# Attention with the keys on the partitions, no transposes of the probabilities, and the value products last in each quarter of a group

## The reference

```
# attention a
q, k, v = (einsum('bsm,hmd->bhsd', ln(x), kernel[i]) for i in range(3))
attn = softmax(einsum('bhsd,bhtd->bhst', q, k) * scale)      # 1024 x 1024 for each head
x = x + einsum(out(attn, v), WO)
# attention b: low-rank projections, and a rotary turn of q and k
q = rope((c_q @ w_up_q.T) ...); k = rope((c_kv @ w_up_k.T) ...); v = c_kv @ w_up_v.T
x = x + (softmax(q k^T / 8) v) @ w_out.T + ln(x)
# rope: even and odd features of a head: e*cos - o*sin, e*sin + o*cos
# FFN: x + gelu(ln(x) @ w1 + b1) @ w2 + b2
```

## Time and profile before

| | us |
|---|---|
| median of 3 runs | 4415.12 |
| profiled execution | 4415.62 |
| its span, first to last instruction | 4413.8 |
| PE busy | 4169.7 (94%) |
| DVE / ACT / POOL busy | 3175.3 / 2636.0 / 780.0 |
| attention a (103 to 2057) / attention b (2404 to 4199) | 1954 / 1795 |
| mean granted TensorE clock | 0.977 |

### The profile page before, as it was taken

One profiled execution on the slowest core, in us unless ns is written; L12 is line 12 of the kernel. 1 busy time (PEld: TensorE's weight loads), 2 busy tenths in 40 slices (PEclk: granted clock), 3 DMA queues, 4 the chain that ended last, 5 costly groups with the idle time before them and its releaser, 6 DMA issues. The chain is left out here.

```text
span 4413.8 us, 82276 instructions
## 1 busy us (share of the span) xinstructions
PE 4169.7 (94%) x26976; PEld 3087.3 (70%) x26976; DVE 3175.3 (72%) x5320; ACT 2636.0 (60%) x4844; POOL 780.0 (18%) x691
## 2 busy tenths in 40 slices
PE   3999999999999999998885999999999999999989
PEld 3777777777777777776773777777777767777678
DVE  5777666776667777675665888888888888888744
ACT  1665555555655565555442666666666666666644
POOL 2000000000000000001222222222222222222111
PEclk9999999999999999999997999999999999999999
DMA  5333332332223332220013333333333333333110
GB/s 178 85 87 87 86 75 65 87 87 63 71 76 87 87 81 71 74 59 24 20 39 107 103 102 99 99 99 99 101 101 101 102 100 102 100 102 99 39 35 24
DMA packets 191926, 364.02 MB, mean 82 GB/s; under 512 B 32833, under 2 KB 57665, under 8 KB 187585
## 3 DMA queue, kind: packets, MB, share of 16 engines
q1 hardware_dynamic: 187456, 351.94, 30.8%
q10 hardware_dynamic: 4224, 8.39, 0.5%
HBM read 104.34 MB, written 20.97 MB: 28 GB/s over the span
## 5 line engine op out<-in xcount | busy, mean ns | idle before, releaser
L837 ACT ACTIVATE a_pT<-a_ps_t 128x512 f32<-128x512 f32 x1024 | 557.5, 595 | 737.8 <-PE a_ps_t L662 737.7
L773 DVE TENSOR_REDUCE a_nmax<-a_ps_s 128x1 f32<-128x1024 f32 x512 | 625.0, 1221 | 389.3 <-PE a_ps_s L652 385.6
L837 ACT ACTIVATE b_pT<-b_ps_t 128x512 f32<-128x512 f32 x1024 | 556.2, 595 | 529.6 <-PE b_ps_t L662 529.6
L773 DVE TENSOR_REDUCE b_nmax<-b_ps_s 128x1 f32<-128x1024 f32 x512 | 623.1, 1217 | 273.7 <-PE b_ps_s L652 272.9
L842 ACT ACTIVATE a_p<-a_ps_s,a_nmax 128x1024 f32<-128x1024 f32 x512 | 572.7, 1119 | 53.4 <-DVE a_nmax L773 50.4
L842 ACT ACTIVATE b_p<-b_ps_s,b_nmax 128x1024 f32<-128x1024 f32 x512 | 572.5, 1118 | 40.1 <-DVE b_nmax L773 35.2
L678 PE MATMUL b_ps_o<-b_pT,b_v 128*64 128x256 f32 x4096 | 555.1, 392 | 1.5 <-issue 1.0
L678 PE MATMUL a_ps_o<-a_pT,a_v 128*64 128x256 f32 x4096 | 555.3, 392 | 1.0 <-issue 1.0
L662 PE MATMUL a_ps_t<-ident,a_p 128*128 128x128 f32 x4096 | 540.2, 276 | 3.5 <-DVE a_p L777 3.5
L662 PEld LDWEIGHTS a_ps_t<-ident,a_p 128*128 128x128 f32 x4096 | 486.4, 142 | 76.8 <-DVE a_p L777 4.8
L662 PE MATMUL b_ps_t<-ident,b_p 128*128 128x128 f32 x4096 | 531.6, 273 | 4.6 <-DVE b_p L777 4.4
(11 more groups left out here) (154 smaller groups left out, 6300.2 us busy)
## 6 DMA issues: line engine op xcount, KB each, us to landing
feat<-feat_a SPq DMA_DIRECT2D x16, 2048.0 KB, 7.8
a_q_h<-a_nat_h SPq DMA_DIRECT2D x256, 128.0 KB, 2.3
a_q_l<-a_nat_l SPq DMA_DIRECT2D x256, 128.0 KB, 2.4
feat<-feat_b SPq DMA_DIRECT2D x16, 2048.0 KB, 9.3
b_partner<-b_plain SPq DMA_DIRECT2D x256, 128.0 KB, 2.0
b_q_h<-b_nat_h SPq DMA_DIRECT2D x256, 128.0 KB, 2.3
b_q_l<-b_nat_l SPq DMA_DIRECT2D x256, 128.0 KB, 2.3
a_k_s<-a_nat_h SPq DMA_DIRECT2D x128, 128.0 KB, 2.3
```

Source lines behind the costliest of these rows:

```text
L773: dve.reduce_max(nmax[:, c % NM:c % NM + 1], ps_s[:, c % 2, :], AX_X, negate=True).then_inc(s_max, 1)
L837: act.activation(pT[:, g % 2, head, 4 * h:4 * h + 4, qi * P:(qi + 1) * P], ps_t[:, h, :, :], ACT.Copy).then_inc(s_tev, 1)
```

## The change

The function `attention` is rewritten; the FFNs and the features' first layer stay.

- Scores with the keys on the partitions: 128 keys x 512 queries of one head (`scores`), two products each, over 128 rows. A row of constant ones in `k2` against a row of -max in `q2` subtracts the maximum inside the product. So the exponentials (ACT, 128x512) come out in the layout that the value products want; the transposes, their copies, and the passes of DVE over p are gone.
- The maxima come from extra products with the queries on the partitions (`maxima`), high parts only, 64 rows each; DVE reduces them (L780), and SP brings them to one row of `q2` by DMA (`shift`).
- The sums: POOL adds the eight tiles of p (`pool_window`, seven 128x1024 additions a group), PE sums over the keys with a product by ones (`row_sums`), and reciprocal, spreading over partitions and the product with o follow, by four DMAs, DVE and POOL.
- The output projection of 512 queries is four plain float32 products in place of twelve in fp32r.
- The rotary turn is done by DVE in PSUM (`rotate`), four operations, without swaps by DMA.
- A group is now 512 queries of two heads; a window u is a group; a body has four windows, a window has four quarters b. In `pe_window` a quarter is: maxima, scores, maxima, projections, output projection, values of the quarter before, row sums.
- ACT converts high parts and keeps v; DVE makes low parts.

```diff
@@ attention: PE @@
+        def maxima(pe, t, c):
+            ...
+            pe.wait_ge(s_red, due(t, 32, c))
+            cols = slice(qi, BLOCK, BT)
+            pe.matmul(ps_x[:, 0, :], q1[0:D, slot, head, cols], k1[0:D, pair % 2, head, 0:BLOCK],
+                      start=True, stop=True).then_inc(s_m, 1)
+            pe.matmul(ps_x[:, 1, :], q1[D:P, slot, head, cols], k2[D:P, pair % 2, head, BLOCK:S],
+                      start=True, stop=True).then_inc(s_m, 1)
+        def scores(pe, t, u, b):
+            if b == 0:
+                pe.wait_ge(s_shift, due(t, 128, 32 * (u + 1)))
+            for i in range(4):
+                pe.wait_ge(s_exp, due(t, 64, e - (0, 3, 3, 2)[i]))
+                pe.matmul(ps_s[:, i % 3, :], k1[:, par, head, keys], q1[:, slot, head, :], start=True, stop=False)
+                pe.matmul(ps_s[:, i % 3, :], k2[:, par, head, keys], q2[:, slot, head, :],
+                          start=False, stop=True).then_inc(s_s, 1)
+        def out_project(pe, t, g, half):
+            ...
+            pe.wait_ge(s_x, due(t, 8, 2 * g + half))
+        def project_qk(pe, t, u, n):
+            ...
+            pe.wait_ge(s_nat_l, due(t, 8, n))
+        def project_v(pe, t, u, n):
+            if n % 2 == 0:
+                pe.wait_ge(s_nat_l, due(t, 8, 2 * u + 8))
+            ...
         def pe_window(pe, t, u):
-            for s in range(STEPS):
-                    scores(pe, t, c)
-                    transposes(pe, t, c - T_LAG)
-                    out_project(pe, t, u, s, g)
-                    project_qk(pe, t, u, s, unit_steps[s])
-                    project_v(pe, t, u, s, v_at(t)[s])
-                    pv(pe, t, g, j)
+            for b in range(4):
+                c = 8 * (u + 1) + 2 * b + 1
+                if live(t, 32, c, 8 * NGROUP):
+                    maxima(pe, t, c)
+                if live(t, 4, u, NGROUP):
+                    scores(pe, t, u, b)
+                if live(t, 32, c + 1, 8 * NGROUP):
+                    maxima(pe, t, c + 1)
+                n = units(u, b)
+                if n is not None and live(t, 8, n, 4 * NPAIR):
+                    project_qk(pe, t, u, n)
+                n = v_units(u, b)
+                if n is not None and live(t, 1, 1, BODIES):
+                    project_v(pe, t, u, n)
+                if b >= 2 and live(t, 4, u - 2, NGROUP):
+                    out_project(pe, t, u - 2, b - 2)
+                w, bb = (u, b - 1) if b else (u - 1, 3)
+                if live(t, 4, w, NGROUP):
+                    values(pe, t, w, bb)
+                if b == 1 and live(t, 4, u - 1, NGROUP):
+                    row_sums(pe, t, u - 1)
@@ attention: DVE @@
+        def rotate(dve, t, n):
+            dve.wait_ge(s_unit, due(t, 8, n + 1))
+            dve.tensor_tensor(turn[0:D, :], ps_t[D:P, 0, :], sin_t[D:P, cols], ALU.mult).then_inc(s_turn, 1)
+            dve.tensor_tensor(turn[D:P, :], ps_t[0:D, 0, :], sin_t[0:D, cols], ALU.mult).then_inc(s_turn, 1)
+            dve.wait_ge(s_turn, due(t, 32, 4 * n + 2))
+            dve.tensor_tensor(ps_t[:, 0, :], ps_t[:, 0, :], cos_t[:, cols], ALU.mult).then_inc(s_turn, 1)
+            dve.wait_ge(s_turn, due(t, 32, 4 * n + 3))
+            dve.tensor_tensor(ps_t[:, 0, :], ps_t[:, 0, :], turn[:], ALU.add).then_inc(s_turn, 1)
+        def dve_window(dve, t, u):
+            for b in range(4):
+                ...
+                    reduce(dve, t, c)
+                if b == 3 and live(t, 4, u - 1, NGROUP):
+                    ...
+                    dve.reciprocal(rqi[:], rq[:]).then_inc(s_recip, 1)
+                if converting and rope is not None:
+                    rotate(dve, t, n)
+                if converting and rope is None:
+                    convert_lo(dve, t, n)
+                    ...
+                    reduce(dve, t, c + 1)
+                if converting and rope is not None:
+                    convert_lo(dve, t, n)
+                if b == 3 and live(t, 4, u - 2, NGROUP):
+                    add_out(dve, t, u - 2, 0)
+                ...
@@ attention: POOL, SP @@
+                        pool.tensor_tensor(out, p[:, 0, 0, :], p[:, 0, 1, :], ALU.add).then_inc(s_sum, 1)
+                    ...
+                            pool.tensor_tensor(out, out, p[:, bb, i, :], ALU.add).then_inc(s_sum, 1)
+            pool.memset(k2[0:D, :, :, :].bitcast(F32), 0.0).then_inc(s_init, 1)
+            pool.memset(q2[0:D, :, :, :].bitcast(F32), 0.0).then_inc(s_init, 1)
+            if u == 0 and live(t, 1, 1, BODIES) and live(t, 1, 0, BODIES):
+                sp.dma_start(feat[:].bitcast(F32), scratch[source].bitcast(F32)).then_inc(s_feat, 16)
+            if live(t, 4, u + 1, NGROUP):
+                sp.wait_ge(s_red, due(t, 32, 8 * (u + 2)))
+                shift(sp, u + 1, 0)
```

More of the change, by code:

```diff
@@ new lines, in maxima @@
+        def maxima(pe, t, c):
+            g, qi, head = c // 8, (c % 8) // 2, c % 2
+            pair, slot = g // 2, g % 4
+            if c % 8 == 0:
+                if g % 2 == 0:
+                    for half in range(2):
+                        pe.wait_ge(s_stack[half], due(t, 2 * SD, SD * (pair + 1)))
+                pe.wait_ge(s_stack[2 + g % 2], due(t, 2 * SD, SD * (pair + 1)))
+            pe.wait_ge(s_red, due(t, 32, c))
[4 more added lines that the diff above has]
+                      start=True, stop=True).then_inc(s_m, 1)
@@ new lines, in values @@
+        def values(pe, t, w, b):
+            par = (w // 2) % 2
+            pe.wait_ge(s_exp, due(t, 64, 16 * w + 4 * (b + 1)))
+            if b == 0:
+                pe.wait_ge(s_oraw, due(t, 4, w))
+                if par == 1:
+                    pe.wait_ge(s_vmove, due(t, 1, w // 4 + 1))
+            if par == 0:
+                pe.wait_ge(s_v, due(t, 8, 8 * (w // 4) + 2 * (b + 1)))
+            for i in range(2):
+                kt = 2 * b + i
+                for head in (i, 1 - i):
@@ new lines, in out_project @@
+        def out_project(pe, t, g, half):
+            par = (g // 2) % 2
+            pe.wait_ge(s_norm, due(t, 4, g + 1))
+            pe.wait_ge(s_wor, due(t, 32, 16 * (g // 2 + 1)))
+            if half == 0:
+                pe.wait_ge(s_rb, due(t, 4, g + 2 if live(t, 4, g + 1, NGROUP) else g + 1))
+            pe.wait_ge(s_x, due(t, 8, 2 * g + half))
+            for i in range(2):
+                qi = 2 * half + i
+                mm = pe.matmul(ps_t[:, 1, i * E:(i + 1) * E], o[:, g % 2, qi * P:(qi + 1) * P], wo[:, par, :],
+                               start=True, stop=True)
+            mm.then_inc(s_o, 1)
@@ new lines, in convert_lo, with add_out @@
+        def convert_lo(dve, t, n):
+            half, which = n % 2, (n % 4) // 2
+            dve.wait_ge(s_nat_h, due(t, 8, n + 1))
+            dve.scalar_tensor_tensor(nat_l[:, half, :], ps_t[:, 0, :], scale if which == 1 else 1.0,
+                                     nat_h[:, half, :].bitcast(F32), ALU.mult, ALU.subtract).then_inc(s_nat_l, 1)
+        def add_out(dve, t, g, half):
+            dve.wait_ge(s_o, due(t, 8, 2 * g + half + 1))
+            body = t + g // 4
+            xs = tile_of(x, (body // (PAIRS // 2)) * KT + 4 * (g % 2) + 2 * half, 2)
+            dve.tensor_tensor(xs, xs, ps_t[:, 1, :], ALU.add).then_inc(s_x, 1)
@@ L953, in attention, with run @@
+        def run(eng, window):
+            for u in range(4):
+                window(eng, -1, u)
+            for u in range(4):
+                window(eng, 0, u)
+            with eng.Fori(1, BODIES - 1) as t:
+                for u in range(4):
+                    window(eng, t, u)
+            for u in range(4):
+                window(eng, BODIES - 1, u)
+            for u in range(3):
+                window(eng, BODIES, u)
         block = ctx.enter_context(nc.Block())
@@ L1020, in rope_tables @@
     sin = np.concatenate([np.sin(freqs), np.sin(freqs)], -1)[:, ::2]
[L1021 to L1023 removed]
+    row = np.arange(P)
+    sign = np.where(row < D, 1.0, -1.0).astype(np.float32)
+    pick = (row % D) // 2
     return np.ascontiguousarray(np.stack([cos.T[pick], sin.T[pick] * sign[:, None]]).astype(np.float32))
```

632 lines of the change are left out of this document (272 added, 360 removed).

## The result

The changed kernel takes 5045.1 us (median of 4 runs, 5038.1 to 5051.7) against 4414.3 for the kernel before beside it (4405.5 to 4417.0): a ratio of 1.143, with a 95% interval of 1.141 to 1.146. I had said 4850, from 4560 to 5040. The sign and the mechanism were right, the size was not: +622 us of span where I had +438. The profiled execution took 5038.1 us.

A forecast was written before the change was run, and what follows sets the result against it. PE's work and the waits PE meets were taken as the bound. Bodies -165 and +200, clock +192 and +35, DMA +108, edges +68 gave +438 on 4415.6 us: 4850 us, range 4560 to 5040.

The forecast's parts named there:

- The sign and the mechanism: Whole kernel: slower, chance 0.87, because PE stands waiting for DVE with ready value products queued behind.
- PE's own work: PE in both attentions without waits: bodies of 102.4 us in a and 94.2 in b, some 16.5 less than before.
- M: Price on PE of a pair of 64-row maxima products running side by side: 0.37 us, bounds 0.37 and 0.58.
- rival C: Maxima on PE run one after the other, 0.21 us more each: +94 and +80 us, 5025 us; chance 0.15.
- 8x0.23+0.11 = 1.95: Price on PE of a quarter's eight score products, 0.11 of it for edges: 1.95 us.
- The values' place: PE queue: ready values wait behind operations needing DVE; stalls of 3.6 us in b, 0.6 to 2.0 in quarter 3.
- The clock: TensorE's clock falls behind stalls: 2.0 us lost per 3.6 us stall, +192, and +35 for gaps of 2.0.
- Rival B: Stalls come as computed, but the clock holds amid dense work: 4590 us; chance 0.17.
- Feat and the shifts: Window 0's feat reload delays the next window's shifts: stall of 5.2 us in b, 15 times, +108 with clock.
- POOL as a bound: POOL's additions take 3.4 us and more, over 31 us a group: 4950 to 5100 us; chance 0.04.
- Edges: Starts and ends of the attentions: +22 and +30 us before the first score, +8 at each end; +68 in all.
- the old loop's edge: Loop-edge time of the earlier kernel, kept in the forecast for both attentions: 50 us in a, 27 in b.

The follow-up runs named there:

- max_same_rows: Changed kernel with both products of a maxima pair in the same 64 rows of the array, one after the other; one execution, 5280.9 us.
- max_contiguous: Changed kernel with, in attention a alone, 128 neighbouring columns of q as maxima weights instead of every fourth; one execution, 5005.1 us.
- values_ahead: Changed kernel with PE's value products moved ahead of the projections and output projection; 4588.4 us, 1.040 times the kernel before.
- dve_early: Changed kernel, values last: DVE's rotation and add_out before the first reduce, nat_l before the second, ACT's nat_h rounding before exponentials; 4419.8 us, 1.001 times the kernel before.
- feat_early: Changed kernel with SP issuing the reload of feat some 8 us earlier, ahead of the next window's shifts; one execution, 4982.4 us.
- sums_left_out: Changed kernel with POOL's row sums left out, its additions nearly emptied (row sums wrong); one execution, 5042.7 us.
- best_a: Changed kernel with values ahead of projections, DVE's rotation and add_out ahead of the first reduce, and feat issued early; 4541.6 us, 1.029 times the kernel before.
- act_between: Changed kernel, values last, DVE's chain reordered, feat issued early, ACT's nat_h rounding and v copies behind the first exponential; 4433.4 us, 1.003 times the kernel before.
- max_full_rows: Changed kernel with each product of a maxima pair over all 128 rows instead of 64; one execution, 5043.0 us.

## Why the prediction was wrong in size

**PE's own work: the step that failed.** "M, a pair of maxima products over 64 rows each: 0.37 (one pass 0.22, the rest for start and edge)". They run side by side, 3 to 4 ns apart, as I took them, but a pair costs 0.555: the pass 0.23 and 0.33 of edges, where I had 0.15. I had taken the edges from the values of the earlier trace rows, whose weights are contiguous, and rival C had the right price (0.58) by the wrong mechanism. Shown by max_same_rows (an added product costs 0.23) and max_contiguous (0.12 of the edge is the stride of the load). 502 pairs a stage by 0.185 are 93 us in a and 93 in b. The same edges sit on the scores, "8x0.23+0.11 = 1.95", which took 2.084: 256 by 0.134, 34 us each. Together 254, of the 251 by which the term was off; what else is in it cancels (values, row sums and v projections came out a little dearer, and a few blocks stand ahead of the first score). The range had no room for this: above C it held the bounds of the stages' edges and of DMA alone. The Trainium skill (TensorEngine Tiling, Key Properties) says that a change of tiling mode drains the array. The trace agrees in that every change costs something: the last product ahead of it takes 0.09 us longer. I took it to be the same small edge everywhere, and these runs don't bear that out: the first product behind a change takes another 0.10 or 0.24, by the load of its weights.

**The values' place: right.** Stalls of 3.46 us for a forecast of 3.6, 91 of them in b for 96; 2.0 us in quarter 3 for 2.0; 0.6 and 1.1 for 0.6 and 1.3. Released by nat_l and by x, as named. values_ahead made them 1.6 us short and dve_early took them away, each by another road, so this is shown.

**The clock: right.** I had 2.0 us behind each stall of 3.6, 257 in all with feat. By the same blocks, the low clock cost 1.9 us behind a stall of 3.5 on the mean, and 1.6 behind the 30 of 2.0 in b; that is some 245 us in b with the 21 behind the feat waits, and some 25 in a. Rival B, that it holds amid dense work, is out.

**Feat and the shifts: right place, 49 us for 78** (12 of 15 waits were 2.7 us, where I had 5.2), since PE comes to the scores 6.3 us behind feat's issue, where I had 4.3 (feat issued at 3361.77, PE there at 3368.08 and held until 3370.74). feat_early shows the cause.

**POOL as a bound: rightly given 0.04.** sums_left_out.

**Edges.** The starts fit. From the last score to the first transfer of the FFN it is 37.2 us in a, where the kernel before took 18.2: 19 more, for a forecast of 8. I had priced the spread like the small transfers beside it, and it takes 9.5 us. That is read from the traces; no run changed the spread. On the other side the changed kernel doesn't show the rest of the old loop's edge that I had kept. That this hides in the kernel's longer lead of projections is my guess, not tested.

## To carry along

In an in-order queue, ready work behind a waiting instruction costs the whole wait, but the same place can be the cover under which the waited-for chain runs: first ask where that chain can start (dve_early, best_a), then where the ready work goes. Price a small product by the edges it adds on both sides, with the weight load of its own layout, and count them: 1,000 times 0.18 us was the error. When the engine's waits are gone, look at what the shorter period does to the transfers: the waits for the shifts were 54 us in the changed kernel, and 127, 81 and 114 in values_ahead, best_a and act_between.

## What the hardware did that I had not expected

- A change of tile between two products costs on both sides: the last product ahead of it takes 0.09 us longer, the first behind it 0.10 where its 128 weight columns are contiguous and 0.24 where they are every fourth one (loads of 184 to 197 and 305 ns). Without a change of tile even the strided load is hidden (max_full_rows: loads of 308 and 320 ns, 0.23 from start to start).
- Granted clock within 7 us behind a gap of PE in attention b: 91 of 91 gaps of 3.5 us were followed by 0.50, and 30 of 30 of 2.0; of 90 gaps of 1.6 in values_ahead one was, but 20 of 61 of the same length in best_a; of 30 of 1.1, none. In attention a it was 17 of 30 gaps of 2.0. So the length of the gap alone doesn't decide.
- A 2 MB transfer through another queue no longer holds the transfers of the first (63 to 0.3 us of waits), but slows those under way beside it (7.0 us to landing for 3.4).
